# Expert stage of a decoder kernel: first product with its output turned, from a copy of the tile's weight

## The reference, cut to what matters

```python
xn = (x - mu) * jax.lax.rsqrt(var + EPS) * gamma + beta
logits = jnp.einsum('btd,ed->bte', xn, router_w)
probs = jax.nn.softmax(logits / TEMP, axis=-1)
w, idx = jax.lax.top_k(probs, K)                       # K = 2 of E = 8
wdense = jnp.sum(jax.nn.one_hot(idx, E, dtype=w.dtype) * w[..., None], axis=-2)
h = jax.nn.silu(jnp.einsum('btd,edf->betf', xn, W1))   # W1: 8 x 256 x 1024
y = jnp.einsum('betf,efd->betd', h, W2)                # W2: 8 x 1024 x 256
out = jnp.einsum('bte,betd->btd', wdense, y)
return out + res
```

## Time and profile before

| | us |
|---|---|
| median of three runs | 3400.73 |
| span of the profiled execution (first to last instruction) | 3399.2 |
| lowest and highest run | 3398.74, 3401.56 |
| TensorE busy | 3002.1 (88% of the span) |
| VectorE busy | 1799.6 (53%) |
| ScalarE busy | 1368.2 (40%) |
| GpSimd busy | 1139.2 (34%) |
| loop over the 39 tiles, from its first matmul to its last | 2106.5 to 2421.7 of the span |

### The profile page before, as it was taken

How to read it: one execution, slowest core, us unless ns; L and a number is a source line. 1 busy time by engine, 2 the same in 40 slices (tenths; PEclk the granted TensorE clock), 3 DMA queues, 4 the chain that set the end, 5 groups by cost and what they waited for, 6 DMA issues and landing times. The chain is left out here.

```text
span 3399.2 us, 47089 instructions
## 1 busy us (share of the span) xinstructions
PE 3002.1 (88%) x17554; PEld 1930.5 (57%) x17554; DVE 1799.6 (53%) x2965; ACT 1368.2 (40%) x2304; POOL 1139.2 (34%) x995
## 2 busy tenths in 40 slices
PE   7779999999999979999988795999687878899877
PEld 6645555555555438888874564766465565344345
DVE  6656565565655654224229654111256758666565
ACT  3334444444444434324323462333232635355554
POOL 0126565665666650000006331333133413121232
PEclk9889999999999989999999896999898899799989
DMA  1100000000000001111100107221200100000000
GB/s 56 53 1 1 1 1 1 1 1 1 1 1 1 1 15 57 50 32 56 50 23 0 35 1 254 34 35 32 53 2 7 28 7 10 2 1 1 1 29 29
DMA packets 108641, 81.89 MB, mean 24 GB/s; under 512 B 22283, under 2 KB 102181, under 8 KB 108421
## 3 DMA queue, kind: packets, MB, share of 16 engines
q1 hardware_dynamic: 94693, 65.15, 6.3%
q0 software_dynamic: 7488, 9.48, 1.7%
q10 hardware_dynamic: 6240, 4.26, 0.4%
HBM read 68.31 MB, written 11.47 MB: 23 GB/s over the span
## 5 line engine op out<-in xcount | busy, mean ns | idle before, releaser
L787 POOL TENSOR_TENSOR acc<-acc,pf 128x512 f32<-128x512 f32 (+1 forms) x448 | 564.0, 1281 | 255.2 <-ACT pf L914 255.2
L971 DVE TENSOR_REDUCE mxa<-ps 128x1 f32<-128x512 f32 x512 | 327.0, 680 | 229.9 <-PE ps L833 227.9
L914 ACT ACTIVATE pf<-ps 128x512 f32<-128x512 f32 x512 | 277.9, 595 | 318.8 <-PE ps L808 293.4
L821 PE MATMUL ps<-pf,v 128*64 128x512 f32 (+1 forms) x1152 | 311.6, 619 | 0.0
L3635 ACT ACTIVATE pT<-ps 128x1024 f32<-128x1024 f32 (+1 forms) x192 | 154.1, 811 | 130.4 <-PE ps L3553 129.8
L3647 DVE TENSOR_REDUCE mx<-ps 128x2 f32<-128x1024 f32 (+1 forms) x192 | 174.8, 950 | 42.4 <-PE ps L3540 36.7
L1168 POOL TENSOR_TENSOR x<-x,ys 128x256 f32<-128x256 f32 x16 | 11.8, 738 | 509.0 <-DVE ys L1373 509.0
L833 PE MATMUL ps<-kH,qH 64*128 64x512 f32 x512 | 158.1, 442 | 23.7 <-DVE mc L979 18.5
L1786 POOL TENSOR_TENSOR e<-e,sm 128x1232 f32<-128x1232 f32 x48 | 107.9, 2247 | 174.6 <-DVE sm L2050 174.6
L2495 DVE TENSOR_SCALAR ys<-ps,xs 128x256 f32<-128x256 f32 x39 | 18.9, 484 | 251.4 <-PE ps L2314 251.4
L811 PE MATMUL ps<-qH,kH 64*128 64x512 f32 (+1 forms) x576 | 144.3, 475 | 1.5 <-ACT pf L914 0.8
(11 more groups left out here) (554 smaller groups left out, 6959.6 us busy)
## 6 DMA issues: line engine op xcount, KB each, us to landing
w_raw<-in_c_h SPq DMA_DIRECT2D x32, 512.0 KB, 4.0
w1a<-in_f_w SPq DMA_DIRECT2D x8, 1024.0 KB, 13.8
w2a<-in_f_w SPq DMA_DIRECT2D x8, 1024.0 KB, 12.8
w_raw<-in_c_w SPq DMA_DIRECT2D x32, 128.0 KB, 2.2
x<-in_x SPq DMA_DIRECT2D x1, 2048.0 KB, 8.4
moe_rows<-rowbuf ACTq DMA_DIRECT2D x4, 512.0 KB, 10.4
moe_acc<-x ACTq DMA_DIRECT2D x1, 2048.0 KB, 13.1
x<-moe_acc SPq DMA_DIRECT2D x1, 2048.0 KB, 8.2
```

What stands on the lines that cost most here:

```text
L787: pool.tensor_tensor(now[0:r, :], now[0:r, :], pf[0:r, n % RING, a, :], ALU.add).then_inc(added.sem, 1)
L821: ins = pe.matmul(g.bk(3)[SIDE[a], :], v[0:r, u // 2 % 2, t, u % 2 * P + a * HD:u % 2 * P + (a + 1) * HD], pf[0:r, n % RING, a, :], start= ...
L914: act.activation(pf[0:r, n % RING, a, :], g.bk(bk.bank[f"s{n}_{a}"])[0:r, :], ACT.Exp, bias=bias)\
L971: dve.tensor_reduce(mxa[:, q % 2, half, a, j:j + 1], g.bk(4 + a), AXX, ALU.max).then_inc(bk.release(f"m{q}_{i}_{a}"), 1)
```

## The change

The first product is computed with its output already turned: for each of the 8 blocks of 128 hidden columns and both halves of the 256 inputs, a 128 x 128 block of the first weight is stationary and the tile's 128 turned rows `xT` are moving. That gives 16 matmuls of 128 columns a tile in place of 4 of 512. A block of hidden columns comes out with the hidden index on the partitions, so the eight transposes of `turn_hidden` go, and ScalarE's Silu writes `hT` directly; the two copies from banks 2 and 3 go too. The first product now alternates between banks 0, 1 and 2, 3. The stationary operand is not taken from `w1a` at an address in a register: VectorE first copies the tile's weight (128 x 2048) to one of two fixed buffers `w1s`, which reuse `h` and `zT`, and TensorE waits for the copy (`w1_copied`, in the order's rows `expert_copied`).

```diff
         h, hT = sb("h", [P, KD, H]), sb("hT", [P, 2, HB, P])
+        w1s = [h[:], zT[:].rearrange("p a k n -> p (a k n)").rearrange("p (k n) -> p k n", n=H)]
-                fills += [(f"a{i}_0", 0), (f"a{i}_1", 1)]
+                fills += [(f"a{i}_0", 2 * (i % 2)), (f"a{i}_1", 2 * (i % 2) + 1)]
-                fills += [(f"h{i}_0", 2), (f"h{i}_1", 3)]
...
-                def hidden(i, e):
+                def hidden(i):
                     pe.wait_ge(*bk.read(f"x{i}", 0))
+                    pe.wait_ge(*w1_copied.at(0, i + 1))
                     for half in range(2):
+                        out = g.bk(2 * (i % 2) + half)
                         pe.wait_ge(*bk.free(f"a{i}_{half}", 0))
-                        for k in range(KD):
-                            ins = pe.matmul(g.bk(half), xT[:, i % 2, k, :],
-                                            w1a[:, ds(e * KD + k, 1), half * CH:(half + 1) * CH].rearrange("p a n -> p (a n)"),
-                                            start=k == 0, stop=k == KD - 1)
-                        ins.then_inc(bk.fill(f"a{i}_{half}"), 1)
-
-                def turn_hidden(i):
...
+                            for k in range(KD):
+                                ins = pe.matmul(out[:, f * P:(f + 1) * P], w1s[i % 2][:, k, at:at + P], xT[:, i % 2, k, :],
+                                                start=k == 0, stop=k == KD - 1)
+                        ins.then_inc(bk.fill(f"a{i}_{half}"), 1)
...
-                            act.wait_ge(*bk.full(f"h{i - 2}_{half}", 0))
-                        act.activation(h[:, i % 2, half * CH:(half + 1) * CH], g.bk(half), ACT.Silu).then_inc(bk.release(f"a{i}_{half}"), 1)
+                            act.wait_ge(*bk.full(f"y{i - 2}", 0))
+                        act.activation(hT[:, i % 2, half * (HB // 2):(half + 1) * (HB // 2), :],
+                                       g.bk(2 * (i % 2) + half).rearrange("p (f s) -> p f s", s=P), ACT.Silu).then_inc(bk.release(f"a{i}_{half}"), 1)
                     if i + 1 < N:
                         rows_out(i + 1)
-                    act.activation(hT[:, i % 2, 0:HB // 2, :], g.bk(2).rearrange("p (f s) -> p f s", s=P), ACT.Copy).then_inc(bk.release(f"h{i}_0"), 1)
...
+                def copied(i):
+                    e = dve.value_load(texp[0:1, i:i + 1], min_val=0, max_val=E8 - 1)
+                    if i >= 2:
+                        dve.wait_ge(*bk.full(f"a{i - 2}_1", 0))
+                    dve.tensor_copy(w1s[i % 2], w1a[:, ds(e * KD, KD), :]).then_inc(w1_copied.sem, 1)
+                    return e
+
+                dve.wait_ge(*w_in.at(0, 32 * E8))
+                own = {i: copied(i) for i in range(2)}
+                for i in range(N):
+                    if i and i + 1 < N:
+                        own[i + 1] = copied(i + 1)
+                    weighted(i, own.pop(i))
```

More of the change, by code:

```diff
@@ L2182, in stage_l1_ffn @@
         xs, xT = sb("xs", [P, RING, MOE_ROW]), sb("xT", [P, 2, KD, P])
-        h, hT = sb("h", [P, 2, H]), sb("hT", [P, 2, HB, P])
+        h, hT = sb("h", [P, KD, H]), sb("hT", [P, 2, HB, P])
         ys = sb("ys", [P, 2, D])
@@ L2201, in stage_l1_ffn @@
                 fills += [(f"y{i - 1}", 4 + (i - 1) % 2)]
-            if i < N:
-                fills += [(f"h{i}_0", 2), (f"h{i}_1", 3)]
         bk = Banks(g, fills)
@@ L2214, in stage_l1_ffn @@
         row_in = [g.ev(f"row_loaded{r}", 16 * len(range(r, N, RING))) for r in range(RING)]
-        y_added = g.ev("y_added", 16 * N)
+        y_added, w1_copied = g.ev("y_added", 16 * N), g.ev("expert_copied", N)
         wide = lambda a: a.unsqueeze(2).broadcast_to([P, NT, E8])
@@ L2288, in turn_rows @@
                     ins.then_inc(bk.fill(f"x{i}"), 1)
-                def hidden(i, e):
+                def hidden(i):
                     pe.wait_ge(*bk.read(f"x{i}", 0))
+                    pe.wait_ge(*w1_copied.at(0, i + 1))
                     for half in range(2):
+                        out = g.bk(2 * (i % 2) + half)
                         pe.wait_ge(*bk.free(f"a{i}_{half}", 0))
-                        for k in range(KD):
-                            ins = pe.matmul(g.bk(half), xT[:, i % 2, k, :],
-                                            w1a[:, ds(e * KD + k, 1), half * CH:(half + 1) * CH].rearrange("p a n -> p (a n)"),
-                                            start=k == 0, stop=k == KD - 1)
-                        ins.then_inc(bk.fill(f"a{i}_{half}"), 1)
-                def turn_hidden(i):
-                    for half in range(2):
-                        pe.wait_ge(*bk.read(f"a{i}_{half}", 0))
-                        pe.wait_ge(*bk.free(f"h{i}_{half}", 0))
                         for f in range(HB // 2):
                             at = half * CH + f * P
-                            ins = pe.transpose(g.bk(2 + half)[:, f * P:(f + 1) * P], h[:, i % 2, at:at + P], g.ident[:])
-                        ins.then_inc(bk.fill(f"h{i}_{half}"), 1)
+                            for k in range(KD):
+                                ins = pe.matmul(out[:, f * P:(f + 1) * P], w1s[i % 2][:, k, at:at + P], xT[:, i % 2, k, :],
+                                                start=k == 0, stop=k == KD - 1)
+                        ins.then_inc(bk.fill(f"a{i}_{half}"), 1)
                 def output(i, e):
@@ L2312, in output @@
                         if f % (HB // 2) == 0:
-                            pe.wait_ge(*bk.read(f"h{i}_{f // (HB // 2)}", 0))
+                            pe.wait_ge(*bk.read(f"a{i}_{f // (HB // 2)}", 0))
                         ins = pe.matmul(g.bk(4 + i % 2)[:, 0:D], hT[:, i % 2, f, :],
@@ L2347, in _ @@
                         e = pe.value_load(texp[0:1, i:i + 1], min_val=0, max_val=E8 - 1)
-                        hidden(i, e)
+                        hidden(i)
                     if i + 1 < N:
@@ L2353, in _ @@
                     if i < N:
-                        turn_hidden(i)
                         last = e
@@ L2393, in _ @@
                         if i >= 2:
-                            act.wait_ge(*bk.full(f"h{i - 2}_{half}", 0))
-                        act.activation(h[:, i % 2, half * CH:(half + 1) * CH], g.bk(half), ACT.Silu).then_inc(bk.release(f"a{i}_{half}"), 1)
+                            act.wait_ge(*bk.full(f"y{i - 2}", 0))
+                        act.activation(hT[:, i % 2, half * (HB // 2):(half + 1) * (HB // 2), :],
+                                       g.bk(2 * (i % 2) + half).rearrange("p (f s) -> p f s", s=P), ACT.Silu).then_inc(bk.release(f"a{i}_{half}"), 1)
                     if i + 1 < N:
                         rows_out(i + 1)
-                    act.wait_ge(*bk.full(f"h{i}_0", 0))
-                    if i >= 2:
-                        act.wait_ge(*bk.full(f"y{i - 2}", 0))
-                    act.activation(hT[:, i % 2, 0:HB // 2, :], g.bk(2).rearrange("p (f s) -> p f s", s=P), ACT.Copy).then_inc(bk.release(f"h{i}_0"), 1)
             @block.vector
@@ L2511, in stage_l1_ffn @@
                    weights_made, wheres_made, tiles_hot, valued, turned_val, rows_hot, indexed,
-                   *row_in, y_added):
+                   *row_in, y_added, w1_copied):
             ev.end()
```

## The result

| | before | after |
|---|---|---|
| median of the runs, us | 3400.95 (4 runs, 3398.74 to 3401.56) | 3488.51 (4 runs, 3482.06 to 3495.57) |
| span of the profiled execution | 3399.2 | 3492.2 |
| the expert stage, from its first matmul to that of the next stage | 384.3 | 467.7 |

The changed kernel is slower, by a ratio of 1.0257 (95% interval 1.0238 to 1.0276), 87.6 us in the medians; 3485 was forecast. Of the 93.0 us between the two spans 83.4 lie in the expert stage. The other 9.6 lie in stages that the change doesn't touch, most of it in the attention of layer 3, which took 432.9 us where it had taken 426.1. Over 300 us of that attention the granted clock was 0.92 in place of 0.96, so the clock had a part in it.

The account below looks back on a forecast made before the run. The prediction took the loop to be bound by TensorE. Its terms, -28.9 (TensorE's work), +90.3 (new wait), +22 (clock) and +1.2 (loop's start), summed to +84.6 us, giving 3485 us, with a range of 3458 to 3540.

Parts of the forecast that it names:

- TensorE's work: Loop over tiles: eight transposes go, -0.87 us, first product in 32 records, +0.13; net -0.74 us a tile, -28.9 us.
- The new wait: First product waits for second product, `weighted`, then the copy on VectorE: 2.44 us a tile, 37 times, +90.3 us.
- the copy would stand as the releaser of the gap: Sign in the changed profile: TensorE idle 2.2 us x 37 before the first product, with the copy named as releaser.
- The clock: TensorE's idle gaps in the loop make its clock fall, about once in three tiles at 1.7 us each: +22 us.
- The loop's start: The first two copies, before the loop, may delay GpSimd's first gather by 0 to 2.5 us; taken as +1.2 us.
- The scatter put off by 0.8 us: In the loop the copy delays GpSimd's scatter by 0.8 us, covered by most of a tile; nothing added to the sum.
- The copy did hide: Rival: the copy is done before the preceding second product ends, leaving only TensorE's saving; 3373 us, chance 0.04.
- The slow rate: Rival: VectorE's copy takes 2.27 us instead of 1.24 and the clock falls in every tile; 3564 us, chance 0.06.
- GpSimd first: Rival: the scatter holds what the copy needs from its dispatch, so the copy starts 2.1 us later; 3604 us, chance 0.07.

Follow-up runs that it names:

- e1: Changed kernel with VectorE's copy of tile i+2 placed ahead of `weighted(i)`, so one tile further ahead; 3376.40 us, 0.9930 of the kernel before.
- e6: Changed kernel with 16 unread transposes of the identity on TensorE behind each second product, filling the idle gap; 3466.01 us, 1.0190 of the kernel before.
- e3: Changed kernel with one more VectorE operation, a maximum over 128 x 1024, ahead of the copy from the third tile on; 3596.01 us, 1.0572 of the kernel before.
- e2: Changed kernel with VectorE copying only half of each weight from the third tile on; 3452.47 us, 1.0147 of the kernel before.

## Why the prediction was right

The cause is the one that was forecast: the copy's place in VectorE's queue, and the clock behind it. That the time came within 4 us of the forecast is in part luck, since small misses cancel: the wait was 2 us too small, the clock's term 3 and the loop's start 1 too large, and some 4 us of the median lie in other stages. Step by step:

- **TensorE's work, -0.74 us a tile: right.** e1 gives the sum without anything else: a pace of 7.24 us for 7.98 - 0.74 = 7.24, and 29.0 us in the stage for 28.9. There the 32 records go from 2256.35 to 2259.92, 3.57 us, so the 0.112 us a record taken from another stage's matmuls held. In the changed kernel they take 2259.67 - 2256.03 = 3.64 us, 0.07 more, behind the idle gap.
- **The new wait, +2.44 us x 37: right.** Undisturbed pace 9.74 us against 7.98 - 0.74 + 2.44 = 9.68. Each link was within 0.01: `weighted` to copy 0.77 (0.78 forecast), copy 1.23 (1.24), copy to TensorE 0.10 (0.11); the 0.06 a tile beyond them is the slower start of the first product behind the gap. It was found in the order of VectorE's queue, and sized with rows of the kernel before. Only the sign was wrong that the copy would stand as the releaser of the gap: the profile says "issue". The copy's 1.23 us shows that the one-input operations were the right neighbours of the earlier trace rows.
- **The clock, +22 us: right in cause, and 18.8 measured by e6.** 12 falls in 37 tiles, 1.5 us each, where one in three at 1.7 was forecast. The cause rests on e6, which took away the idle time alone. The rate was a judgement from three gaps of other stages, which gave no rate; that it came out for gaps of 2.26 us is luck in part, and the cost of a fall taken from the same rows was too small in e3.
- **The loop's start, +1.2 us: wrong.** From the start of `put` to the first product 6.35 us passed, 6.65 before. The trace of the changed kernel shows copy and gather at once:

```profile
2098.32 1.62 POOL L2252 DMA_INDIRECT xs<-moe_rows,take  x1 [7.75 <-DVE put L2477]
2098.58 1.23 DVE L2491 COPY h<-w1a 128x2048 f32 x1 [1.19 <-issue]
...
2101.96 0.29 PEld L2286 LDWEIGHTS ps<-ident,xs 128*128 128x128 f32 x2 [6.33 <-DMA xs<-moe_rows,take]
```

  The gather took 1.62 us instead of 1.22, but its rows were there in time: TensorE started 4.76 us after `put` started, 4.97 before.
- **The scatter put off by 0.8 us without a cost: right in effect.** Its record starts as early behind `weighted` as before (1.29 us), but lasts 2.17 us in place of 1.59, so it ends 0.58 us later. What sets its end is the copy: the scatter ends 1.46 us after it (2257.39 and 2255.93), and so it does beside the short copy of e2 (2262.60 and 2261.14). So all but 0.13 us of the scatter's 1.59 come after the copy. e1 has the same 2.17 at full pace, so it costs nothing.
- **The rivals.** The copy did hide in e1, with 29 us gained, for just the reason given: its place ahead of `weighted`. It can't be the changed kernel, since there it stands behind. The slow rate is out (1.23 us). GpSimd first is out: the copies start 0.77 us behind `weighted`, before the scatter.

Sum of the stage: -28.9 + 37 x 2.5 + 19 = 82.6, measured 83.4. The 4 us by which the medians differ more lie in other stages.

## What to carry to other kernels

Read the queue order of the engine that makes an operand, not only the lengths: a 1.2 us copy, on an engine that is idle for over 80% of the loop, cost 112 us of the stage (467.7 against 355.3 in e1), since it stood behind a wait for the very product that it should have been done before. One position in the order turned 2.6% lost into 0.7% gained. When work is taken off the bounding engine, ask what that work was covering. And price an idle gap on TensorE by its clock as well: gaps of 1.7 us cost only themselves in this loop, those of 2.3 us drew a fall in one of three, those of 3.3 us in 35 of 37.

## What the runs showed of the hardware that I had not expected

- An indirect DMA on GpSimd and a 128 x 2048 VectorE copy beside it: the copy took 1.22 to 1.23 us in every case, also where GpSimd's instruction had begun 0.26 or 0.51 us ahead of it (the loop's start, e3). GpSimd's instruction was the one that got longer: the scatter from 1.59 to 2.17 us (1.84 in e3, 1.64 beside the short copy of e2). Casts beside a GpSimd tensor operation went from 0.41 to as much as 1.49 us. The Trainium skill (SBUF — State Buffer, section "SBUF: two separate sides") lets whoever starts first keep the shared ports for its whole instruction. The scatter behind a copy fits that, since nearly all of it comes after the copy's end (above). The indirect DMA ahead of a copy does not: the copy was not held up, and the DMA's instruction ended 0.13 us (loop's start) and 0.11 us (e3) after the copy. It seems to need the ports in parts and not all the time, which was not tested.
- A fall of the clock lasted 3.4 us in the rhythm of 9.7 us and 6.8 us in that of 13.7 us.
